# Positions of a head written and read in four transfers of every second partition, in place of two of all partitions

## The reference

```
def _relative_shift(x):
    b, h, s, _ = x.shape
    x = jnp.pad(x, ((0, 0), (0, 0), (0, 0), (1, 0)))
    x = x.reshape(b, h, s + 1, s)
    return x[:, :, 1:, :].reshape(b, h, s, s)
...
content_score = jnp.einsum('bhsp,bhtp->bhst', q + u, k)
pos_score = jnp.einsum('bhsp,htp->bhst', q + v, pos)
pos_score = _relative_shift(pos_score)
score = (content_score + pos_score) / jnp.sqrt(jnp.float32(P))
weights = jax.nn.softmax(score, axis=-1)
out = jnp.einsum('bhst,bhtp->bhsp', weights, val)
```

## Time and profile before

| | |
|---|---|
| runs, median of 3 | 4684.43 us (4677.82 to 4687.61) |
| profiled execution | 4672.52 us |
| its span, first to last instruction | 4670.4 us |
| mean granted TensorE clock | 0.97 |
| PE busy | 4306.7 us, 92% |
| DVE busy | 3333.9 us, 71% |
| ACT busy | 3199.2 us, 69% |
| POOL busy | 1260.1 us, 27% |
| DMA packets | 474414, 1391.19 MB |

### The profile page before, as it was taken

One profiled execution on the slowest core, in us unless ns is written; L12 is line 12 of the kernel. 1 busy time (PEld: TensorE's weight loads), 2 busy tenths in 40 slices (PEclk: granted clock), 3 DMA queues, 4 the chain that ended last, 5 costly groups with the idle time before them and its releaser, 6 DMA issues. The chain is left out here.

```text
span 4670.4 us, 121633 instructions
## 1 busy us (share of the span) xinstructions
PE 4306.7 (92%) x48308; PEld 3327.4 (71%) x48308; DVE 3333.9 (71%) x8095; ACT 3199.2 (69%) x4124; POOL 1260.1 (27%) x905
## 2 busy tenths in 40 slices
PE   7899999899989989999998999889999999999997
PEld 3466666666666666666666666678888888888886
DVE  7688888888888888888887787755555555544455
ACT  3588888888888888888888888744444444444454
POOL 0111111111111111111111111135556666544443
PEclk9899999999999999999999999999999999999998
DMA  9999999999999999999999999973555555433268
GB/s 342 343 394 391 398 380 399 389 386 390 389 384 397 385 391 389 384 398 387 389 388 387 391 388 394 381 250 58 134 134 128 135 127 134 108 55 86 46 188 297
DMA packets 474414, 1391.19 MB, mean 298 GB/s; under 512 B 65408, under 2 KB 142848, under 8 KB 473728
## 3 DMA queue, kind: packets, MB, share of 16 engines
q1 hardware_dynamic: 424704, 1316.27, 74.4%
q0 software_dynamic: 49152, 67.14, 8.7%
HBM read 708.93 MB, written 674.23 MB: 296 GB/s over the span
## 5 line engine op out<-in xcount | busy, mean ns | idle before, releaser
L761 DVE CUSTOM_DVE_ANT_0 att_shifted<-att_quad,att_shifted 128x512 f32<-128x512 f32 x2048 | 1346.5, 685 | 479.4 <-PE att_quad L987 308.8
L600 ACT ACTIVATE ring<-att_quad 128x1024 f32<-128x1024 f32 x1024 | 1051.2, 1027 | 219.5 <-PE att_quad L976 195.3
L608 ACT ACTIVATE att_pt<-att_tp 128x1024 f32<-128x1024 f32 x1024 | 1048.6, 1024 | 13.5 <-PE att_tp L1009 10.6
L768 DVE TENSOR_SCALAR att_shifted<-att_shifted,att_mn 128x512 f32<-128x512 f32 x2048 | 1032.8, 545 | 0.0
L987 PE MATMUL att_quad<-att_kd,att_qd 64*128 64x512 f32 x2048 | 880.5, 462 | 131.9 <-DVE att_mn L761 118.9
L976 PE MATMUL att_quad<-att_pos,att_qd 64*128 64x512 f32 x2048 | 840.6, 444 | 93.5 <-ACT ring L600 86.9
L1427 ACT ACTIVATE ffn_hp<-ffn_up 128x512 fp32r<-128x512 f32 x512 | 306.2, 598 | 855.1 <-PE ffn_up L1607 853.5
L1512 DVE TENSOR_TENSOR ffn_hp<-ring,ffn_hp 128x512 fp32r<-128x512 f32 x512 | 383.9, 750 | 617.9 <-ACT ring L1429 615.5
L1008 PEld LDWEIGHTS att_tp<-ident,att_shifted 64*128 64x128 f32 x8192 | 673.9, 142 | 210.2 <-DVE att_shifted L768 135.2
L1008 PE MATMUL att_tp<-ident,att_shifted 64*128 64x64 f32 x8192 | 763.1, 230 | 54.1 <-ACT att_pt L608 37.5
L1607 PE MATMUL ffn_up<-ffn_xp,ffn_w1p 128*128 128x512 f32 x3072 | 794.3, 394 | 2.8 <-DVE ffn_xp L1456 2.8
(11 more groups left out here) (132 smaller groups left out, 5222.7 us busy)
## 6 DMA issues: line engine op xcount, KB each, us to landing
xs_d<-ring SPq DMA_DIRECT2D x1024, 513.0 KB, 7.8
att_shifted<-xs_d SPq DMA_DIRECT2D x1024, 512.0 KB, 8.2
att_shifted<-in_L_attn_x_dram SPq DMA_DIRECT2D x32, 512.0 KB, 6.8
xn_d<-att_shifted SPq DMA_DIRECT2D x32, 512.0 KB, 6.2
xt_d<-att_shifted SPq DMA_DIRECT2D x32, 512.0 KB, 7.4
gathered<-xt_d SPq DMA_DIRECT2D x32, 512.0 KB, 10.2
att_d<-att_osb SPq DMA_DIRECT2D x512, 32.0 KB
ring<-in_L_ffn_w_dram SPq DMA_DIRECT2D x16, 1024.0 KB, 7.7
```

Source lines behind the costliest of these rows:

```text
L600: act.activation(xo[:, kk % NW, 2 * half:2 * half + 2, 1:S + 1], xp[:, :, :], ACT.Copy).then_inc(x_out, 1)
L608: act.activation(turned_keys(n, half), tp[:, :, :].rearrange("p r (k n) -> p k r n", k=2 * TT), ACT.Exp, scale=-1.0).then_inc(t_out, 1)
L761: dve.tensor_tensor_reduce(out=shifted[:, kk % NX, t], in0=sp_[:, t % 2], in1=shifted[:, kk % NX, t], scale=-0.25, scalar=-NEG, op0=ALU.ad ...
L768: dve.tensor_scalar(shifted[:, kk % NX, t], shifted[:, kk % NX, t], mn[:, kk % NX, t:t + 1], None, ALU.subtract).then_inc(lowered, 1)
```

## The change

Each half (two of the four rows) of a head is written and read by two transfers instead of one: first the even partitions, then the odd ones. SP's order for a head becomes write, read, write, read, ... over four quarters: (half 0, even), (half 0, odd), (half 1, even), (half 1, odd). Only the first quarter waits for the slot, the first of each half for ACT's evacuation. All waits for `x_written` and `x_shifted` count 64 a head instead of 32.

```
-                def write_x(i, kk, half):
+                def write_x(i, kk, half, odd):
 
                     slot, turn = of_slot(kk)
-                    if half == 0:
-                        wait_alone(sp, x_shifted[slot], (i * (BH // NX) + turn) * 32)
+                    if half == 0 and odd == 0:
+                        wait_alone(sp, x_shifted[slot], (i * (BH // NX) + turn) * 64)
                     rows = slice(2 * half, 2 * half + 2)
-                    wait_alone(sp, x_out, (i * BH + kk) * 2 + half + 1)
-                    sp.dma_start(xs_d[slot].rearrange("(p t c) -> p t c", t=TT, c=S + 1)[:, rows], xo[:, kk % NW, rows]).then_inc(x_written[slot], 16)
-
-                def read_x(i, kk, half):
+                    if odd == 0:
+                        wait_alone(sp, x_out, (i * BH + kk) * 2 + half + 1)
+                    dst = xs_d[slot].rearrange("(p two t c) -> two p t c", two=2, t=TT, c=S + 1)[odd]
+                    sp.dma_start(dst[:, rows], xo[odd::2, kk % NW, rows]).then_inc(x_written[slot], 16)
+
+                def read_x(i, kk, half, odd):
 
                     slot, turn = of_slot(kk)
-                    if half == 0:
-                        wait_alone(sp, x_written[slot], (i * (BH // NX) + turn + 1) * 32)
+                    if half == 0 and odd == 0:
+                        wait_alone(sp, x_written[slot], (i * (BH // NX) + turn + 1) * 64)
 
                         wait_alone(sp, t_full, (i * BH + kk - NX + 1) * TT)
                     rows = slice(2 * half, 2 * half + 2)
-                    sp.dma_start(shifted[:, slot, rows], xs_d[slot][S:S + S * S].rearrange("(p t c) -> p t c", t=TT, c=S)[:, rows]
-                                 ).then_inc(x_shifted[slot], 16)
+                    src = xs_d[slot][S:S + S * S].rearrange("(p two t c) -> two p t c", two=2, t=TT, c=S)[odd]
+                    sp.dma_start(shifted[odd::2, slot, rows], src[:, rows]).then_inc(x_shifted[slot], 16)
...
                     for kk in range(BH):
-                        for half in range(2):
+                        for half, odd in ((0, 0), (0, 1), (1, 0), (1, 1)):
                             if not (last and kk + LEAD - 1 >= BH):
-                                write_x(i, kk + LEAD - 1, half)
+                                write_x(i, kk + LEAD - 1, half, odd)
                             if not (last and kk + LEAD - 1 - BEHIND >= BH):
-                                read_x(i, kk + LEAD - 1 - BEHIND, half)
+                                read_x(i, kk + LEAD - 1 - BEHIND, half, odd)
```

More of the change, by code:

```diff
@@ L433, in _ @@
                             sp.wait_ge(xt_stored[n], 16 * (B // NS))
-                    for half in range(2):
-                        write_x(0, k, half)
+                    for half, odd in ((0, 0), (0, 1), (1, 0), (1, 1)):
+                        write_x(0, k, half, odd)
                         if k >= BEHIND:
-                            read_x(0, k - BEHIND, half)
+                            read_x(0, k - BEHIND, half, odd)
                 load_xt(1)
@@ L455, in body @@
                             for k in range(NX):
-                                sp.wait_ge(x_written[k], B * H // NX * 32)
+                                sp.wait_ge(x_written[k], B * H // NX * 64)
                             load_first(sp, w1, 0, w1s).then_inc(shared.w1_in, 16)
@@ L597, in x_evacuate @@
                         slot, turn = of_slot(kk - NW)
-                        act.wait_ge(x_written[slot], (i * (BH // NX) + turn + 1) * 32)
+                        act.wait_ge(x_written[slot], (i * (BH // NX) + turn + 1) * 64)
                     act.wait_ge(x_full, (i * BH + kk) * 2 + half + 1)
@@ L758, in add @@
                         slot, turn = of_slot(kk)
-                        wait_alone(dve, x_shifted[slot], (i * (BH // NX) + turn + 1) * 32)
+                        wait_alone(dve, x_shifted[slot], (i * (BH // NX) + turn + 1) * 64)
                     wait_alone(dve, s_full, n * TT + t + 1)
```

## The result

The changed kernel takes 5078.55 us in the median (5065.63 to 5080.74, 4 runs) against 4685.58 us before: a ratio of 1.084, interval 1.083 to 1.086. That is 393 us slower, where 19.5 us had been forecast, and outside the range. The profiled execution has a span of 5078.6 us.

A forecast was written before the change was run, and what follows sets the result against it. The prediction took the DMA engines to bound the attention phase. Only small packets cost anything, +19.5 us, all else nothing: 4684.4 + 19.5 = 4704 us, with a range of 4655 to 4780.

The forecast's parts named there:

- What bounds the kernel: Attention phase: the DMA engines are never without a packet (share 1.01), so a head takes its packets' time, 5.59 us.
- Data packets: Position-score writes and reads: twice the transfers of half the partitions, the same packets a head; cost nothing.
- completion packets: DMA engines: 16 small packets an issue, 32768 more at 9.5 ns over 16 engines, +19.5 us (0 to 39).
- SP's issues: SP's queue: four more issues a head, 1.5 us more, covered by its waits; cost nothing.
- The cover: SP's queue: its waits of 2.81 us a head absorb the extra issues, and queued transfers cover a late one.
- The backlog of six transfers: DMA queue: about six 0.5 MB transfers are queued at any moment, which covers a late issue.
- Order on SP: SP: one quarter instead of a half goes ahead of the wait for a landed write; the engines don't run dry, nothing.
- start and end: From 130 to 200 us first quarters may go sooner or later, nothing within 2 us; after 3040 us nothing changes.
- SP becomes the bound: SP's queue: issues over 0.63 us on average decide the time; +307 us at 0.70 throughout; chance 0.08.
- its partial case: SP's queue: SP also waits for others in between, so +50 to +100 us, 4760 us; within the 0.08 chance.
- Ports: SBUF: engines sharing a port slow each other's packets, up to +440 us, 5125 us; chance 0.05.
- Evening-out: DMA engines: finer turns of writes and reads lift the mean rate, 36 us gained, about 4660 us; chance 0.16.

The follow-up runs named there:

- experiment 1: Changed kernel with only the writes by quarters, the reads left as halves as in the kernel before: 4702.27 us, ratio 1.0045 to the kernel before.
- the trains: Transfers issued back to back on SP at the very start, then waited for, added to the kernel before: 0.596 us an issue of 64 partitions, 0.432 of 128.
- experiments 6: Stores of outputs and sums moved from SP's queue to GpSimd's: 4838.44 us from the changed kernel, 4688.35 us from the kernel before (ratio 1.0026).
- experiment 9: Kernel before with eight small transfers a head added on SP, 4 partitions of 512 B each: 5057.02 us, ratio 1.081.
- experiment 4: Kernel before with back-to-back transfers of several shapes added at its start, mostly 16 of each: some 150 us longer, a whole time that says nothing.

## Why the prediction was wrong

*What bounds the kernel.* Right for before: with a DMA share of 1.01, nothing but more work on the engines or a slower supply could slow it. That SP supplies them was named and then set aside.

*Data packets, completion packets.* The counts held exactly (32768 more), and the price nearly: the trace's records give 9 ns for a small packet, before and after, against the 9.5 put in. Halving the upper bound of 19 ns was a guess that came out. The 13 to 29 us of experiment 1 hold more than small packets. This term was right; the slowdown comes from the next.

*SP's issues: the step that failed.* It read "2 x 0.32 + 2 x 0.43 = 1.5 us more a head ... Cost: nothing". The medians came from issues of 128 partitions, the 0.32 us also from ones with a pause before them (back to back 128 take 0.43). An issue of 64 takes 0.60 us and 0.04 of gap: in the trains, without other traffic, 8 x 0.64 + 0.66 = 5.8 us a head, already over the 5.59 of the DMA engines. That explains about 0.2 us a head, 100 us in all. In the running kernel the head took 6.33 us, or 0.71 an issue. Against 5.59 that is 0.74 us x 512 = 379 of the 393 us; so the larger part comes from issues that last longer in traffic than in the trains, and what makes them longer is not shown. That SP's issuing is what bounds the kernel is shown by experiments 6 and 9; of its price only the part in the trains is explained by the shape. No row of the trace before holds an issue of 64 partitions. I had bounded it by its nearest rows, 0.46 to 0.50 at 4 to 16 partitions and 0.32 to 0.43 at 128, as if the price had to lie between them.

*The cover.* "SP's waits of 2.81 us a head cover it": four more at 0.71 would be 2.8 us alone, and the four old ones became dearer too, from 0.44 to 0.64 us on average by the issue records, another 0.8 us a head. "The backlog of six transfers" is still six, but of half the bytes, so it covers half the time.

*Order on SP, start and end.* Not visible: the wait for `x_written` has vanished from SP's list, since SP comes so late that all has landed. From 130 to 200 us the DMA share is 0.85 as before.

*The rivals.* "SP becomes the bound" was the right one, with the right decision point (0.63 us an issue) and price (+307 us at 0.70); it had a chance of 0.08 and only its partial case was in the range. Ports: refuted for every second partition by 396 GB/s in experiment 4 and by the packets' medians. Evening-out: no sign in any run; the one with finer turns and a waiting SP (1) was 0.45% slower. Its sum in the prediction is off by a little: 4684 - 36 + 0 to 39 is 4648 to 4687, not 4650 to 4665; nothing hangs on it.

## What to carry to other kernels

Before splitting a transfer, add up what the issuing queue spends: number of issues times the price back to back, which is seen in trains without pauses and not in medians of a queue that waits. Take even that as a lower bound: here the trains gave 0.64 us an issue and the kernel 0.71. Where the DMA engines are full and the queue has slack, more issues cost little (four small ones a head: 0.45%) until their sum passes the engines' time, and then all of it shows (eight: 8%). Price the very shape that the change will use: half the partitions was dearer to issue than all.

## What was not expected of the hardware

- With rows of 512 B, an issue on SP takes 0.295 us with 4 or 8 partitions, 0.42 to 0.43 with 16 to 48 and 80 to 128, but 0.60 with 64 (neighbouring or every second) and with 32 taken every fourth. 64 every second also take 0.60 with 4096 B, written or read. Why is open.
- Written in a train of 4096 B rows, 64 every-second partitions move 396 GB/s, 64 neighbouring ones 206 GB/s.
- In the running kernel issues take longer than in the trains (from the start of one to the start of the next 0.71 against 0.64 us), in part through single ones of over 1 us, such as 1.53 us at 2002.74 us. What holds SP in them was not tried. In the trains it was held only where the DMA engines were full.
- Where SP is the bound, more of the reads' packets take over 250 ns (2.4% before, 6.5% after, 7.2% in experiment 9), at an unchanged median of 159 ns.
- Packets of 8 KB gave no higher rate than packets of 4 KB in this traffic: 386 against 390 GB/s.
